# Neighbour sums as two float32r passes, spare chunks by gathered rows, and x written out and reloaded, in a one-core graph layer

## The reference, cut to what matters

```
xn = layernorm(x)                                   # 1250 nodes x 512
neigh = segment_sum(xn[src], dst)                   # 40000 edges, float32
rst   = (1 + eps) * xn + neigh
gnn   = relu(rst @ W1 + b1) @ W2 + b2 + xn
mix   = attention of xn with relu(q k^T) v, 8 heads of 64, @ W_out + b_out
x     = x + gnn + mix
x     = x + experts(layernorm(x))                   # top 2 of 16 experts
```

## Time and profile before

| | us |
|---|---|
| runs | 841.29 (median of 3), 840.32 the lowest |
| the profiled execution, its own time | 841.39 |
| its span, first to last instruction | 839.6 |
| TensorE busy | 756.8 (90%) |
| VectorE busy | 429.2 (51%) |
| ScalarE busy | 216.3 (26%) |
| GpSimd busy | 133.0 (16%) |
| mean granted TensorE clock | 0.949 of full speed |

### The profile page before, as it was taken

How to read it: one execution, slowest core, us unless ns; L and a number is a source line. 1 busy time by engine, 2 the same in 40 slices (tenths; PEclk the granted TensorE clock), 3 DMA queues, 4 the chain that set the end, 5 groups by cost and what they waited for, 6 DMA issues and landing times.

```text
span 839.6 us, 11824 instructions
## 1 busy us (share of the span) xinstructions
PE 756.8 (90%) x3591; PEld 440.4 (52%) x3592; DVE 429.2 (51%) x1330; ACT 216.3 (26%) x446; POOL 133.0 (16%) x191
## 2 busy tenths in 40 slices
PE   4989999999999999999989999999997799999900
PEld 2545544454545545455444446768785166666700
DVE  4536743566757667576972124334545523233325
ACT  2311211232313323132222105051341024343400
POOL 5054440000000000000830000002202100000054
PEclk9989999999999999999999999999997579999965
DMA  9100000607063424444233700001118853333367
GB/s 296 22 0 1 0 2 1 241 11 263 13 252 115 150 101 151 169 146 154 110 141 122 292 10 0 1 0 76 51 45 323 327 226 112 133 110 132 112 189 228
DMA packets 44871, 101.38 MB, mean 121 GB/s; under 512 B 6652, under 2 KB 6668, under 8 KB 42384
## 3 DMA queue, kind: packets, MB, share of 16 engines
q1 hardware_dynamic: 40048, 81.16, 27.0%
q0 software_dynamic: 3616, 11.17, 4.2%
q10 hardware_dynamic: 1152, 8.39, 2.5%
HBM read 42.17 MB, written 58.54 MB: 120 GB/s over the span
## 4 chain that ended last, share of the span: by engine, by line
PE 83%; DVE 6%; POOL 3%; issue 3%; DMA 2%; ACT 1%; SPq 0%; POOLq 0%; DVEq 0%
PE bank L1149 10%; PE bank L1069 10%; PE bank L1132 9%; PE bank L1100 8%; PE bank L1240 7%; PE bank L1186 7%; PE bank L1301 7%; PE bank L1040 6%; PE bank L1314 6%; PE bank L1111 4%; PE bank L1171 4%; POOL arena L563 2%; PE bank L1277 2%; DVE arena L802 2%; DMA arena<-in_wqkv 2%
## 5 line engine op out<-in xcount | busy, mean ns | idle before, releaser
L802 DVE TENSOR_SCALAR arena<-iota,arena 125x128 f16<-125x128 f16 x392 | 120.7, 308 | 80.8 <-PE bank L1040 71.2
L804 DVE TENSOR_SCALAR arena<-iota,arena 125x320 f16<-125x320 f16 x392 | 131.2, 335 | 0.0
L633 ACT ACTIVATE arena<-bank 128x416 f32<-128x416 f32 (+1 forms) x120 | 62.2, 518 | 186.0 <-PE bank L1132 182.9
L825 DVE TENSOR_SCALAR arena<-bank 128x416 f32<-128x416 f32 (+1 forms) x120 | 69.1, 591 | 68.1 <-PE bank L1132 68.1
L1149 PE MATMUL bank<-arena 128*64 128x416 f32 (+1 forms) x480 | 97.2, 525 | 1.6 <-DVE arena L825 1.6
L1069 PE MATMUL bank<-arena 128*128 128x512 f32 x200 | 96.2, 605 | 0.0
L1040 PE MATMUL bank<-arena 125*128 125x320 f16 x392 | 72.1, 301 | 7.4 <-DVE arena L804 6.7
L1100 PE MATMUL bank<-arena 128*128 128x416 f32 (+1 forms) x192 | 75.8, 544 | 2.8 <-DMA arena<-in_wqkv 1.4
L1240 PE MATMUL bank<-arena 128*128 128x384 f32 (+2 forms) x256 | 70.3, 430 | 0.0
L1040 PEld LDWEIGHTS bank<-arena 125*128 125x128 f16 x392 | 35.8, 98 | 60.0 <-issue 36.2
L1301 PEld LDWEIGHTS bank<-arena 128*128 128x128 f32 x448 | 53.1, 198 | 17.4 <-issue 15.7
(11 more groups left out here) (205 smaller groups left out, 940.5 us busy)
## 6 DMA issues: line engine op xcount, KB each, us to landing
slots<-arena SPq DMA_DIRECT2D x6, 5376.0 KB, 16.4
slots<-arena SPq DMA_DIRECT2D x2, 5120.0 KB, 15.4
arena<-in_ew SPq DMA_DIRECT2D x8, 1024.0 KB, 10.2
arena<-in_ew ACTq DMA_DIRECT2D x8, 1024.0 KB, 12.4
arena<-slots SPq DMA_DIRECT2D x32, 256.0 KB, 2.7
slots<-arena SPq DMA_DIRECT2D x28, 256.0 KB, 2.0
arena<-in_gw SPq DMA_DIRECT2D x2, 2048.0 KB, 10.2
arena<-in_wqkv SPq DMA_DIRECT2D x3, 1024.0 KB, 16.1
```

What stands on the lines that cost most here:

```text
L633: act.activation(probs[0:kt, s % NPB, 0, 0:n], bank[2 * (s % 2)][0:kt, 0:n], ACT.Relu).then_inc(p0_ready, 1)
L802: dve.tensor_scalar(ring[:, at_slot:at_slot + P], iota16[0:CE, 0:P], window_cols[:, i % WBUF, 1, k:k + 1], None, ALU.is_equal)
L804: dve.tensor_scalar(ring[:, at_slot + P:at_slot + OHW], iota16[0:CE, :], window_cols[:, i % WBUF, 0, k:k + 1], None, ALU.is_equal).then_in ...
L825: dve.tensor_single_scalar(probs[0:kt, s % NPB, 1, 0:n], bank[2 * (s % 2) + 1][0:kt, 0:n], 0.0, op=ALU.max).then_inc(p1_ready, 1)
```

## The change

Four things, and what they need:

- **Two passes.** `xn_hi` is `xn` rounded to float32r (ScalarE, one tile a turn in turns 8 to 17), `xn_lo` = xn - xn_hi (VectorE, one tile a turn, a turn later, in the place of `xn`). `a_t` becomes a float32r tensor. Each of the 100 sum products becomes two float32r products of the same shape. `rst` takes two chained VectorE instructions, one for `xn_hi`, one for `xn_lo`.
- **Spare chunks** no longer go through the counts: GpSimd works out each edge's source row, gathers these rows of `xn` from memory with an indirect transfer and makes a 125 x 128 one-hot of targets; TensorE multiplies these two before the last product of the group. All of it is inside the branch that is taken only where there is a spare chunk. The branches themselves move: on TensorE from between two windows to ahead of the last sum product of the group (two branches there), on GpSimd to the group's sum turn.
- **The base sums** (L539, L540) go from the end of GpSimd's window work to directly behind L467.
- **Two round trips.** SyncE writes `xn` to `xn_rows` once `xn` is ready, and `xr` (with the base sums) to `base_rows` once those are made. `xn_hi` lies where `xr` lay: ScalarE waits for both transfers at turn 8. After the last `rst` SyncE reloads `xr`; the additions of L835 wait for that instead of `base_ready`.

```diff
+    xn_rows = nc.dram_tensor("xn_rows", [NT * P, D], f32, kind="Internal").ap()
+    base_rows = nc.dram_tensor("base_rows", [NT * P, D], f32, kind="Internal").ap()
...
+        XR = VT + 4 * NT * D
         xn = at(XN, [NT, D])
-        zeros = at(RINGB + 10752, [D])
-        a_t = at(A_T, [2, NT, P])
+        xn_lo, xn_hi = ([split_tensor(f"{name}{t}", at_byte + 4 * D * t, [D]) for t in range(NT)]
+                        for name, at_byte in (("xn_lo", XN), ("xn_hi", XR)))
+        zeros = at(RINGB + 12288, [D])
+        a_t = split_tensor("a_t", A_T, [2, NT, P])
...
-                    pe_after[used(made)] += [("pair", w, k), ("spare", w - 1), held]
+                    pe_after[used(made)] += [("pair", w, k), held]
...
+                summed.append(used(made) + 3 + (NT - 1) // 2)
... SyncE
+            sp.wait_ge(xn_ready, NT)
+            sp.dma_start(xn_rows.rearrange("(t p) d -> p t d", p=P), xn[:, :, :]).then_inc(xn_stored, 16)
+            sp.wait_ge(base_ready, NT)
+            sp.dma_start(base_rows.rearrange("(t p) d -> p t d", p=P), xr[:, :, :]).then_inc(base_stored, 16)
             sp.wait_ge(zeros_ready, 1)
...
+            sp.wait_ge(rst_ready, NT)
+            sp.dma_start(xr[:, :, :], base_rows.rearrange("(t p) d -> p t d", p=P)).then_inc(base_in, 16)
             sp.wait_ge(av_step, NS)
... GpSimd
+            for t in range(NT):
+                pool.wait_ge(xn_ready, t + 1)
+                link(pool.tensor_tensor(xr[:, t, :], xr[:, t, :], xn[:, t, :], ALU.add))
+                link(pool.tensor_tensor(xr[:, t, :], xr[:, t, :], bias_b2[:, :], ALU.add))
+                pool.sem_inc(base_ready, 1)
+
             pool.wait_ge(edge_ps, 1)
...
                 with pool.If(both > 0):
+                    pool.wait_ge(xn_stored, 16)
... in the branch, per spare chunk: ten small tensor_scalar and a copy for row and target, then
+                        pool.indirect_dma_start(
+                            out=spare_rows, out_offset=None, in_=xn_rows,
+                            in_offset=bass.IndirectOffsetOnAxis(ap=spare_i[:, :], axis=0)).then_inc(spare_in, 16)
+                        pool.tensor_scalar(spare_to, iota16[0:CE, 0:P], to, None, ALU.is_equal).then_inc(spare_ready, 1)
...
-                                     + [(start(w), "spare", w) for w in range(0, NW, 2)]):
+                                     + [(summed[w // WPG], "spare", w) for w in range(0, NW, 2)]):
...
-            for t in range(NT):
-                link(pool.tensor_tensor(xr[:, t, :], xr[:, t, :], xn[:, t, :], ALU.add))
-                link(pool.tensor_tensor(xr[:, t, :], xr[:, t, :], bias_b2[:, :], ALU.add))
-                pool.sem_inc(base_ready, 1)
... ScalarE, after saving product g
+                if HIGH_FROM <= g < HIGH_FROM + NT:          # HIGH_FROM = 8
+                    if g == HIGH_FROM:
+                        act.wait_ge(base_stored, 16)
+                        act.wait_ge(xn_stored, 16)
+                    t = g - HIGH_FROM
+                    act.activation(xn_hi[t][:, :], xn[:, t, :], copy).then_inc(xn_hi_ready, 1)
                 graph(g)
... VectorE
-                    dve.scalar_tensor_tensor(out=rst, in0=xn[:, i, :], scalar=eps1[:, 0:1], in1=bank[NB][:, :],
-                                             op0=ALU.mult, op1=ALU.add).then_inc(rst_ready, 1)
+                    link(dve.scalar_tensor_tensor(out=rst, in0=xn_hi[i][:, :].bitcast(f32), scalar=eps1[:, 0:1],
+                                                  in1=bank[NB][:, :], op0=ALU.mult, op1=ALU.add))
+                    dve.scalar_tensor_tensor(out=rst, in0=xn_lo[i][:, :].bitcast(f32), scalar=eps1[:, 0:1],
+                                             in1=rst, op0=ALU.mult, op1=ALU.add).then_inc(rst_ready, 1)
...
             for turn in range(FROM, NPRE):
+                if HIGH_FROM < turn <= HIGH_FROM + NT:
+                    t = turn - HIGH_FROM - 1
+                    dve.wait_ge(xn_hi_ready, t + 1)
+                    dve.tensor_tensor(xn_lo[t][:, :], xn[:, t, :], xn_hi[t][:, :].bitcast(f32),
+                                      ALU.subtract).then_inc(xn_lo_ready, 1)
...
-                dve.wait_ge(base_ready, t + 1)
+                dve.wait_ge(base_in, 16)
... TensorE: count_spare becomes spare_sums, whose body is
+                                pe.matmul(bank[NB][:, :], spare_to, spare_rows, start=False, stop=False,
+                                          skip_group_check=True).then_inc(spare_used, 1)
... neighbours(g, t)
+                    pe.wait_ge(xn_lo_ready, NT)
+                if t == NT - 1:
+                    for w in range(g * WPG, g * WPG + WPG, 2):
+                        spare_sums(w)
-                ins = pe.matmul(bank[NB][:, :], a_t[:, g % 2, t, :], xn[:, t, :], start=(t == 0), stop=(t == NT - 1))
+                for x in (xn_hi, xn_lo):
+                    ins = pe.matmul(bank[NB][:, :], a_t[:, g % 2, t, :], x[t][:, :], start=(t == 0 and x is xn_hi),
+                                    stop=(t == NT - 1 and x is xn_lo), skip_group_check=True)
```

More of the change, by code:

```diff
@@ L65 @@
 FAR_DOWN = -3.0e38
+WHOLE = 12582912.0
 FAR = 1000.0
@@ L139, in layer @@
         rst = at(RSTB, [D])
-        spare = at(SPAREB, [OHW // 2], parts=CE).bitcast(f16)
+        spare_rows = at(SPAREB, [D], parts=CE)
+        spare_to = at(SPAREB + 4 * D, [P], parts=CE)
         o_t = at(QT, [PAIRS, N])
@@ L192, in layer @@
         spare_col = sb("spare_col", [CE, 2, 1])
+        spare_f = sb("spare_f", [CE, 4])
+        spare_i = sb("spare_i", [CE, 1], i32)
         bias_b2, bias_bo = sb("bias_b2", [P, D]), sb("bias_bo", [P, D])
@@ L252, in layer @@
         onehots_ready, onehots_used = sem("onehots_ready"), sem("onehots_used")
-        spare_ready, spare_used = sem("spare_ready"), sem("spare_used")
+        spare_ready, spare_used, spare_in = sem("spare_ready"), sem("spare_used"), sem("spare_in")
+        xn_stored, base_stored, base_in, xn_hi_ready, xn_lo_ready = (
+            sem(n) for n in ("xn_stored", "base_stored", "base_in", "xn_hi_ready", "xn_lo_ready"))
         spare_chain, spare_waited = sem("spare_chain"), sem("spare_waited")
@@ L301, in layer @@
         NPRE = NPROJ + NT
+        HIGH_FROM = 8
         PREP, FROM, EARLY = 4, 8, 8
@@ L307, in start @@
             return FROM + w * (NPRE - FROM) / EARLY if w < EARLY else NPRE + (w - EARLY) * EVERY
+        summed = []
         def used(made):
@@ L515, in spare_window @@
                     pool.reg_mov(chunk, lo + USUAL[w])
+                    code, inside, to, block = (spare_f[:, i:i + 1] for i in range(4))
                     with pool.Fori(0, extra):
@@ L1037, in _ @@
             pe.reg_mov(pairs, 0)
+            landed = pe.alloc_register("pe_landed")
+            pe.reg_mov(landed, 0)
             def product(w, of, at_slot, start, stop):
@@ L1059, in count_spare @@
                                 pe.wait_ge(spare_ready, pe.snap(pairs, min_val=0, max_val=NW * NC) + 1)
-                                product(v, spare, 0, False, False).then_inc(spare_used, 1)
                                 pe.reg_add(pairs, pairs, 1)
+                                pe.reg_add(landed, landed, 16)
+                                pe.wait_ge(spare_in, pe.snap(landed, min_val=16, max_val=16 * NW * NC))
+                                pe.matmul(bank[NB][:, :], spare_to, spare_rows, start=False, stop=False,
+                                          skip_group_check=True).then_inc(spare_used, 1)
             def neighbours(g, t):
@@ L1082, in graph @@
                 for what in pe_after[turn]:
-                    {"pair": count_pair, "spare": count_spare, "sum": neighbours, "turn": turn_sums}[what[0]](*what[1:])
+                    {"pair": count_pair, "sum": neighbours, "turn": turn_sums}[what[0]](*what[1:])
             for g, (which, p, b) in enumerate(projections):
```

17 lines of the change are left out of this document (12 added, 5 removed).

## The result

The change makes the kernel **faster**: 813.74 us (813.19 to 814.98) against 840.81 for the kernel before in the same session, a ratio of 0.9692 with a 95% interval of 0.9673 to 0.9711. The forecast was 804, with 792 to 816 as its range. All comparisons use undisturbed runs; one execution of the kernel before at 1962.9 us and one of experiment 7 at 2504.6 us are left out. The profiled execution took 813.19 us, 811.4 of it span.

The account below looks back on a forecast made before the run. TensorE, busy 90% of the span and carrying 83% of the chain that ended last, was taken as the bound. 841.4 - 43.9 - 5.4 + 10.5 + 1.5 = 804 us, range 792 to 816.

Parts of the forecast that it names:

- passes: TensorE's 100 sums, in attention and the v products, as 200 float32r passes at 0.232 us: -43.9 us.
- the stretch at 400 us: End of attention, 400 to 428 us: GpSimd no longer adds there, so slow pairs shorten: -5.4 us.
- early additions: Base additions from 15 us block VectorE's normalizations, edge work and marks, then the clock falls: +10.5 us, at most 13.
- remainders: Rounding and subtractions in turns 8 to 18, beside the second pair's split; VectorE cannot run ahead: +1.5 us, 0 to 4.
- the second `rst`: Ten more chained VectorE instructions at about 0.74 us, covered by the turns before turning: 0, upper bound 4.5 us.
- the transfers: Writing `xn` and `xr` and reloading after the last `rst` land before they hold anything up: 0.
- branches: Spare-chunk branches, 20 on TensorE, two together ahead of one product: 0 to 3 us, taken as 0.
- the rival of waits: Short sums no longer cover relu and one-hot stores, VectorE sets the pace, half of 43.9 lost: 826 us, chance 0.1.
- the pairs at the rim: Pairs at the edge of the 400 to 428 us stretch: may give 1 or 2 us more, left out of -5.4.
- the marks get through: Blocking by early additions falls only on long or float16 instructions, so +4 instead of +10.5: 796 us, chance 0.18.

Follow-up runs that it names:

- experiment 7: Changed kernel without early additions or writing out `xr`; x and normalized rows reloaded after the last `rst`, added during the output product; subtractions five turns later: 793.38 us.
- experiment 6: Changed kernel with one float32 product per sum, on the rounded rows, in place of the two float32r passes: 853.48 us.
- 5: Kernel before the change with GpSimd's 20 base additions left out altogether: 832.21 us.
- 1: Changed kernel with GpSimd's 20 early base additions left out, every wait, transfer and rounding kept: 803.19 us.
- 2: Changed kernel with the ten remainder subtractions five turns later, behind the split of the second pair: 805.03 us.
- 8: The version of experiment 7 with the sums in runs of four (eight passes) in every second turn: 793.42 us.
- Experiment 3: Changed kernel with VectorE's ten subtractions left out but their waits on ScalarE's roundings kept: 806.21 us.

## Why the prediction was right, and where it was not

The terms as the runs give them: passes -39.7 (experiment 6), the stretch at 400 us -7.2 (5), early additions +10.5 (1), remainders +8.7 (2). They sum to -27.7; measured is 813.74 - 840.81 = -27.1. The 0.6 us left over are within the scatter between sessions, so the second `rst`, the transfers and the branches together cost nothing that can be told; none was tried by itself. The trace of after shows no wait for the transfers: ScalarE's first rounding (61.01 us) follows its save without an idle time, and the output additions wait for TensorE alone. The stages say the same as the runs: -38.8 for the passes, -7.0 at 400 us, +10.4 and +8.5 before attention.

**Sums in two passes: right in kind, 4 to 5 us too large.** The forecast had -43.9 with 0.232 us a pass. TensorE's timeline of after shows that start to start, but only behind the first pass of a run, which takes 0.34:

```profile
208.62 0.50 PE L1127 MATMUL bank<-xn_hi,a_t 128*128 128x512 f32 x1
208.96 0.40 PE L1127 MATMUL bank<-xn_lo,a_t 128*128 128x512 f32 x1
209.19 0.40 PE L1127 MATMUL bank<-xn_hi,a_t 128*128 128x512 f32 x1
209.43 0.39 PE L1127 MATMUL bank<-xn_lo,a_t 128*128 128x512 f32 x1
209.66 0.58 PE L1090 MATMUL bank<-arena 125*128 125x320 f16 x3
```

The term was mis-sized on both sides, because I took pieces of the chain for prices. A pair without sums takes 3.8 us in both kernels. Four sums make it 7.32 before and 5.78 after, so a sum adds 0.88 us before (I had 0.908) and 0.495 after (I had 0.464). A sum saves 0.385 us and not 0.444. Attention says the same: 306.7 - 271.7 = 34.9 us for 90 sums, 0.388 each. The slow first pass of a run behind counts is no fee that could be saved: with half as many runs in attention (8) the time stayed. VectorE kept up: the pair with four sums has TensorE busy in all of it, as the forecast said against the rival of waits.

**The stretch at 400 us: right, 2 us too small.** Predicted -5.4, with 1 or 2 more for the pairs at the rim; measured -7.2. The rim pairs belonged in the sum. Attention shows both terms: 34.9 us of sums and 7.0 make 41.9 of the 42.0 by which it became shorter.

**The additions at 15 us: right in size, by two errors that cancel.** +10.5 was predicted and measured, and the marks were turned at 46.38 us where "about 46" was forecast. But the rule from which I got there (two VectorE instructions per GpSimd instruction, all of them) held for neither end of the work. The long instructions pass one at a time: normalization ended at 30.5, not 27, and the integer and two-input work at 41, not 35. The marks, for which I had eight blocked rounds, met only the last two additions, because they began at 41 and GpSimd was done at 43.55 and not at 47. That the two errors met at 46 us is luck. TensorE's loss is then 8.7 us until L1071 (37.67 to 46.38) and 1.7 in the product behind it, against the 8 and 2.5 of the forecast. The rival "the marks get through" is half right as to the marks and wrong in its sum.

The Trainium skill, page "SBUF — State Buffer", section "Who interferes with whom", says that a blocked instruction waits for the whole of the other one, and that reductions never contend here. The trace agrees with both: L777 takes 1.48 us in after and 0.41 without the additions, while the reductions L783 and L784 take 0.66 us each in the middle of GpSimd's additions (37.60 and 38.19 us) and without them. The page does not decide between one and two instructions per turn; the timeline does.

**Remainders: the step that failed, by 7 us.** The forecast had named the place (VectorE cannot run ahead of ScalarE's turn while the second pair is split) and gave it 1.5 us, 4 at most; it cost 8.7. I had costed the instructions and not the standstill that they end in. Ten subtractions are 8.1 us on an engine with time to spare, and experiment 2 does all of them with next to no idle time of TensorE. What costs is that the waits drain the one-hot store just when GpSimd's 2.8-us instructions block VectorE: two idle times of 2.6 us, and behind them products of 4.33 and 4.32 us instead of 2.96, with 0.79 of the clock granted over 82 to 90 us. The two make 5.3 us of idle time and 2.7 of slower products, 8.0 of the 8.7. Experiment 3 shows that wait and instruction are needed together. The price was in the earlier trace rows: a short idle time of TensorE there already cost nearly its own length again (not in every execution, as the last section says).

Together, by the medians: 804 lacked 7.2 us of remainders and 4.2 of the passes and had 1.8 too much at 400 us, which makes 813.6 where 813.74 was measured.

## What to carry to other kernels

Price a moved GpSimd instruction by what VectorE must finish in its new place; where a later stage has slack, the same 20 additions cost nothing that the times or the trace show (7), against 7 and 10.5 us in the two places tried first. When an engine that fills a store for TensorE gets an extra wait, put it where nothing else delays that engine: turns five later made 8.7 us of difference with no work taken out. The saving on the busiest engine arrived in full at its true price (0.385 us a sum in a pair, 0.388 over attention), so look for the loss in the new side work. Take the price of a piece from two stretches with and without it; here pieces of the chain gave 0.444.

## What the runs showed of the hardware that I had not expected

- Behind back-to-back GpSimd additions of 1.3 us, a VectorE instruction that is short by itself passes in twos (1.26 and 0.25 us for the marks), but the 80 x 500 int32 instructions (0.41 us alone) and the two-input L788 (0.68 alone in experiment 1's kernel, 1.63 in after) pass one at a time.
- 128 x 512 float32r passes run at 0.233 us from start to start, the first of a run behind counts at 0.34. The counts before it take as much less, 0.31 us for three, so half as many runs gained nothing (793.42 against 793.38 us).
- Behind an idle time of TensorE of 2.6 to 4.3 us the next product of eight took 4.3 to 4.7 us in after instead of 2.96, with 0.66 of the clock granted over 84.95 to 89.40 us; in before it was 0.55 over 56 to 62.4 us, nearly all of it at the lower of the two levels, 1.2 GHz. How much a standstill costs is not told by its length. The same 2.8 us ahead of the first counts were followed by a product of 5.29 us in before, 5.34 in 8 and 2.96 in 5 and 7, and idle times of 2.63 us by 5.72 us in 1 and 4.33 in after.
